# When the layer norm's tiles are normalised in a two-layer expert FFN: half 1's first norm one tile per step, half 0's second norm one step earlier

## What is computed

```python
x = x + ffn1(layernorm(x), token_ids, ctx, ctx, ctx)
x = x + ffn2(layernorm(x), Wg, W1, W2, W3)

# ffn1: 4 experts of width 256, chosen by the token's id
y = einsum('bsf,df->bsd', silu(h @ Wg[e].T) * (h @ Wu[e].T), Wd[e])   # Wg = Wu = Wd = ctx
# ffn2: 8 experts of width 176, the best 2 of 8 scores, softmax over the two
h = silu(x @ W1[e].T) * (x @ W2[e].T)
y = y + w[..., e:e + 1] * (h @ W3[e].T)
```

## Time and profile before

| | us |
|---|---|
| median of 3 runs | 166.16 |
| lowest and highest run | 165.45, 166.22 |
| span of the profiled execution | 165.1 |
| PE busy in it | 154.5 |
| DVE busy in it | 114.8 |
| POOL busy in it | 55.9 |

### The profile page before, as it was taken

One profiled execution on the slowest core, in us unless ns is written; L12 is line 12 of the kernel. 1 busy time (PEld: TensorE's weight loads), 2 busy tenths in 40 slices (PEclk: granted clock), 3 DMA queues, 4 the chain that ended last, 5 costly groups with the idle time before them and its releaser, 6 DMA issues.

```text
span 165.1 us, 2425 instructions
## 1 busy us (share of the span) xinstructions
PE 154.5 (94%) x892; PEld 131.7 (80%) x892; DVE 114.8 (70%) x225; ACT 65.1 (39%) x115; POOL 55.9 (34%) x47
## 2 busy tenths in 40 slices
PE   7599799999995999999999999999999999999991
PEld 2177689898982879888888778898888888888890
DVE  0788999955989865799999784945444744444452
ACT  3395557643742431763344432206222222222210
POOL 0599825779796330757464000000000000000000
PEclk9999999999999599999999999999999999999999
DMA  3975325232033000150000000000000300000003
GB/s 104 331 271 173 95 67 142 81 95 81 22 95 95 0 0 4 16 175 0 0 0 4 2 0 0 2 4 0 0 0 0 126 5 0 0 0 4 0 2 127
DMA packets 4332, 8.76 MB, mean 53 GB/s; under 512 B 736, under 2 KB 864, under 8 KB 4320
## 3 DMA queue, kind: packets, MB, share of 16 engines
q1 hardware_dynamic: 4176, 8.60, 16.7%
q10 hardware_dynamic: 144, 0.00, 0.0%
HBM read 7.55 MB, written 1.05 MB: 52 GB/s over the span
## 4 chain that ended last, share of the span: by engine, by line
PE 46%; DVE 17%; issue 14%; POOL 13%; ACT 4%; DMA 3%; SPq 1%; DVEq 0%; POOLq 0%; ACTq 0%
PE z L626 26%; PE y L651 18%; POOL gated L315 9%; DVE act L538 4%; DVE act_lo L503 4%; POOL w_lo L275 3%; DMA raw<-weights_dram 3%; DVE norm L436 2%; DVE x_sb L449 2%; DVE stats L421 2%; DVE gated L528 2%; ACT act_hi L352 1%; ACT w_hi L327 1%; PE y L585 1%; POOL rstd L285 1%
## 5 line engine op out<-in xcount | busy, mean ns | idle before, releaser
L626 PE MATMUL z<-hT_hi,w_hi 128*128 128x512 f32 x120 | 48.0, 400 | 0.6 <-ACT hT_hi L336 0.3
L626 PE MATMUL z<-hT_hi,w_lo 128*128 128x512 f32 x120 | 47.4, 395 | 0.0
L503 DVE TENSOR_TENSOR act_lo<-act,act_hi 128x512 fp32r<-128x512 f32 x38 | 33.4, 880 | 15.0 <-ACT act_hi L352 14.4
L651 PE MATMUL y<-w_hi,act_lo 128*128 128x256 f32 x152 | 43.5, 286 | 0.2 <-DVE act_lo L503 0.2
L651 PE MATMUL y<-w_hi,act_hi 128*128 128x256 f32 x152 | 43.5, 286 | 0.0
L651 PE MATMUL y<-w_lo,act_hi 128*128 128x256 f32 x152 | 43.4, 286 | 0.0
L380 ACT ACTIVATE silu<-z 128x512 f32<-128x512 f32 x38 | 22.7, 597 | 45.2 <-PE z L626 45.2
L626 PE MATMUL z<-hT_lo,w_hi 128*128 128x512 f32 x120 | 37.2, 391 | 0.0
L275 POOL TENSOR_TENSOR w_lo<-raw,w_hi 128x768 fp32r<-128x768 f32 (+1 forms) x15 | 27.4, 1839 | 19.3 <-ACT w_hi L327 19.3
L352 ACT CAST act_hi<-act 128x512 fp32r<-128x512 f32 x38 | 23.5, 618 | 26.0 <-DVE act L538 25.6
L651 PEld LDWEIGHTS y<-w_hi,act_lo 128*128 128x128 f32 x152 | 29.4, 193 | 2.1 <-issue 0.4
(11 more groups left out here) (48 smaller groups left out, 75.3 us busy)
## 6 DMA issues: line engine op xcount, KB each, us to landing
raw<-weights_dram SPq DMA_DIRECT2D x11, 384.0 KB, 3.2
raw<-weights_dram SPq DMA_DIRECT2D x8, 256.0 KB, 4.8
x_sb<-x_dram SPq DMA_DIRECT2D x4, 256.0 KB, 4.6
out_dram<-x_sb SPq DMA_DIRECT2D x4, 256.0 KB, 2.5
consts_sb<-consts_dram SPq DMA_DIRECT2D x1, 68.0 KB, 3.8
ids_sb<-token_ids_dram ACTq DMA_DIRECT2D x1, 4.0 KB, 4.0
router_raw<-router_dram SPq DMA_DIRECT2D x1, 8.0 KB, 2.8
```

The source lines that it names most:

```text
L503: nc.vector.tensor_tensor(act_lo[:, i, :], act[:, i, :], act_hi[:, i, :].bitcast(F32), ALU.subtract)\
L626: return nc.tensor.matmul(bank[:], w[b][:, c, cols], tokens[:, h, k, :], **flags)
L651: last = nc.tensor.matmul(o, a[:, q % BUFFERS, rows], w[b][:, c, wd], start=(first and j == 0), stop=(c == CHUNKS[b] - 1 and j == 2), skip ...
```

## The change

Four entries of the tables move, and one loop of four instructions is taken apart.

- Half 1's first norm: `normalise` no longer issues its four tiles in step 1, but one tile in each of the steps 1, 2, 3 and 4, at the place where `normalise` stood: behind that step's act and its w_lo. Its transposes move from (4, 0) to (5, 0), its `tokens_hi` from step 4 to 5, its `tokens_lo` from step 5 to 6.
- Half 0's second norm: `inverse_deviation` and `normalise` move from step 12 to step 11. Its transposes stay at step 14.
- Weight piece (1, 3) is split at step 14 and no longer at step 12: its w_hi on ACT, its w_lo on POOL.

```diff
-    "inverse_deviation": (1, 4, 5),
-    "normalise": (1, 4, 4),
-    "transpose_tokens": ((4, 0), (6, 0), (6, 1)),
-    "tokens_hi": (4, 5, 6),
-    "tokens_lo": (5, 5, 5),
+    "inverse_deviation": (1, 3, 5),
+    "normalise": (None, 3, 4),
+    "transpose_tokens": ((5, 0), (6, 0), (6, 1)),
+    "tokens_hi": (5, 5, 6),
+    "tokens_lo": (6, 5, 5),
...
-SPLIT_AT |= {6 + 2 * c: (1, c) for c in range(4)}
+SPLIT_AT |= {(6, 8, 10, 14)[c]: (1, c) for c in range(4)}
...
-                for i, t in enumerate(tiles_of(h)):
+                for i, t in [(i, h * HALF_TILES + i) for i in parts]:
...
-                    normalise(bb, hh, (x_sb, x2_sb)[bb])
+                    normalise(bb, hh, x2_sb)
+                if 1 <= q <= HALF_TILES:
+
+                    normalise(0, 1, x_sb, (q - 1,))
```

More of the change, by code:

```diff
@@ L427, in statistics, with normalise @@
                         nc.vector.tensor_scalar(var[:, cols], mv[:, cols, 1], EPS, None, ALU.add).then_inc(var_done, 1)
-            def normalise(b, h, src):
+            def normalise(b, h, src, parts=range(HALF_TILES)):
                 if ln_no(b, h):
                     dve.wait_ge(norm_T, KD * ln_no(b, h))
-                for i, t in enumerate(tiles_of(h)):
+                for i, t in [(i, h * HALF_TILES + i) for i in parts]:
                     dve.wait_ge(rstd_done, ln_part_no(ln_no(b, h), t))
```

## The result

| | before | after |
|---|---|---|
| median of 4 runs, us | 166.19 | 171.92 |
| lowest and highest run | 165.45, 166.40 | 170.73, 173.32 |
| span of the profiled execution | 165.1 | 169.9 |
| ratio, with its 95% interval | | 1.0329 (1.026 to 1.040) |

The change made the kernel 3.3% slower. I had forecast slower, 169.0 us; the time lies 2.9 us above that and 1.5 us above the range. Medians are of all runs, but a ratio, here and in the experiments, is one of mean times without the slow runs (more than 1.5% above the fastest of their kernel). Each ratio is against runs of the kernel before that were made alongside; their medians are 166.19 here, 165.94 for experiments 1 to 4, 166.25 for 5 to 8 and 166.79 for 9 to 12.

The account below looks back on a forecast made before the run. The prediction took PE, busy 154.5 of 165.1 us, as the bound. Half 1's stand +3.3, clock +1.1 and half 0's moves -1.6 put +2.8 on the median 166.16: 169.0 us, range 166.0 to 170.4.

Parts of the forecast that it names:

- The new stand of part 1: At half 1's moved transposes PE waits 4.3 us for the fourth norm tile; down(2) starts at 27.6, +3.3 us.
- the rule used for the 1.4: Old loss at half 1's transposes: 2.2 us until down(1), less 0.8 us estimated for eight transposes without a wait.
- The clock behind it: Granted clock expected to fall after half 1's long stand: +1.1 us, bounds 0 and 1.6.
- hT_lo at up(8): Half 1's later tokens_lo makes hT_lo barely due for up(8): charged nothing with the low clock, 0.3 us without.
- Part 2: Half 0's second norm at step 11, weight piece (1,3) at step 14: 3.9 us won, -1.6 us net at up(17).
- The two waits named for it: PE waits for hT_lo at the scores, 0.9 us, and for gate_rows at the gate's transposes, giving back gain.
- The anchor: Baseline of the sum: span 165.1 to 167.9 us, carried as +2.8 onto the median 166.16, giving 169.0.
- The holds: On DVE, act_lo, w_lo and norm tiles exclude POOL's gated, each for its length, four gated delaying half 1's tiles.
- The one in which the clock stays up: Rival, 22%: the clock stays full in half 1's long stand; 168.2 us (167.4 to 168.7).
- The one with fewer holds: Rival, 13%: half 1's stand costs only +1.9 with the clock up, half 0's moves bring 1.9; 166.2 us.
- the faster case: Rival, 9%: DVE's tiles slip between POOL's instructions in both places; costs 0.3, wins 3.9; 162.6 us (to 165.3).
- the worse one: Rival, 8%: a second low stretch of the clock when the scores wait, +1.6; 170.6 us.

Follow-up runs that it names:

- experiments 1 to 4: Four follow-up kernels: the change's half 1 norm alone, its other moves alone, half 0's earlier norm alone, and the changed kernel with filler matmuls; 172.48, 165.92, 166.88, 169.41 us.
- 5 to 8: Four follow-up kernels: filler in the kernel before, a two-tiles-a-step norm, a later weight piece (1,3), and filler with halved gated; 165.27, 167.33, 166.61, 168.53 us.
- 9 to 12: Four follow-up kernels: weight piece (1,3) at step 14 without and with filler, two-tiles-a-step norm with early rounding, and these combined; 164.78, 164.56, 164.47, 163.48 us.
- after_fill16: Changed kernel plus 16 throwaway matmuls in front of half 1's transposes, where PE stands anyway; 169.41 us, ratio 1.020 to the kernel before.
- part1_only: Changed kernel with half 0's second norm and weight piece (1,3) back at step 12, leaving only half 1's norm moves; 172.48 us, ratio 1.039.
- tiles22: Kernel before with half 1's norm as two tiles in steps 1 and 2, transposes and tokens moved as in the change; 167.33 us, ratio 1.002.
- part2_only: Kernel before with only half 0's second norm at step 11 and weight piece (1,3) at step 14; 165.92 us, ratio 1.001.
- the fifth experiment: The run before_warm, with its table of spans by mean granted clock; 165.27 us, ratio 0.992.
- after_fill10_halfgate: Changed kernel plus 10 filler matmuls before half 1's transposes, with gated(3) to gated(5) on half the columns; 168.53 us, ratio 1.015 to the kernel before.
- piece14_only: Kernel before with only weight piece (1,3) moved from step 12 to 14, both norms staying; 164.78 us, ratio 0.990.
- norm11_only: Kernel before with only half 0's second norm at step 11, weight piece (1,3) staying at step 12; 166.88 us, ratio 1.006.
- before_warm: Kernel before with filler matmuls in the starting warm-up and in front of half 1's first and half 0's second transposes; 165.27 us, ratio 0.992.

## Why the prediction was wrong in size and right in kind

- **The new stand of part 1** was right in its mechanism, and in its number partly by luck. Tile 4 was put at 26.97 and ended at 26.78; down(2) was put at 27.6, +3.3 us, and started at 27.81, +3.45. The 0.65 us from the last tile to down(2) was a full-clock figure and became 1.03 on the low clock. Without it, as after_fill16 shows, down(2) is 3.0 us late. (The wait, put at 4.3 us, is 4.9 - 0.8 = 4.1 by the rule used for the 1.4.)
- **The clock behind it is the term that failed**: +1.1 us with bounds of 0 and 1.6, measured +2.3 (5.16 us against 2.82), and with the 0.4 us in the stand 2.7 in all. I took the worst case from the one low stretch of before, 1.6 us, and deducted what would pass while PE stands. The low level did begin during the stand, at 26.0, but it then lasted 6.8 us and not the 3.4 of before, so 5 us of it fell on PE's work. In part1_only the same stand brought 3.4 us of it and cost 1.1. A bound from a single row was no bound.
- **hT_lo at up(8)** was charged at nothing with the low clock; down(3) to down(5) takes 0.4 us more than before, all of it in up(8), and tiles22's profile names this wait in the same place. The change moved tokens_lo behind the router's remainder, which POOL's w_lo holds.
- **Part 2** was right in the profile: forecast 3.9 won and 2.3 given back, -1.6 net; measured from down(5) to up(17) 6.20 - 4.81 = 1.4. Two misses nearly cancel in it: 3.3 won (1.8 at down(11) instead of 2.3, and 1.5 of clock, 4.43 against 2.92) and 1.9 given back. The two waits named for it are there, 0.7 and 0.6 us. But 1.6 of the 3.9 was the low clock behind the second stand, which 8 of 31 runs of before don't have anywhere. Against those, part2_only is 0.3 us slower.
- **The anchor.** The sum was made on a span of 165.1 and put on the median 166.16 as a difference. Every run has 1.8 us outside its span, so the profiled execution stood for 166.9 us, 0.7 above that median: the 11 runs with its mean clock of 0.99 in the fifth experiment's table span 164.2 to 165.0, and it is slower than each of them. The changed kernel's span and median agree (169.9 + 1.8 = 171.7, and 171.92). So +4.8 in span became +5.7 between the medians. In the span the forecast was 2.0 us too low: 1.2 by the clock, 0.4 by hT_lo, 0.2 by part 2 and 0.15 by down(2). The clock term alone would have put the time at 170.2, still inside the range; with the anchor it is outside.
- **The holds.** That DVE's w_lo waits for POOL's gated, on which the 3.3 us rest, is borne out by after_fill10_halfgate; that tiles are held by POOL's work, by piece14_only (2.02 us for four instead of 3.51). The Trainium skill ("SBUF — State Buffer", Who interferes with whom) says that a DVE instruction with two SBUF inputs contends with a GpSimd instruction that reads SBUF; the w_lo of 0.98 and 0.68 us beside the halved gated, in place of 1.18 and 1.15, agree. One reading of the prediction needs care: by the earlier trace rows the third tile starts at 18.96, before gated at 19.04, and yet it is the tile that is held, so the recorded starts don't tell which of the two got in first.
- **The rivals.** The one in which the clock stays up fell for the profiled run, and none of the four has a full clock: their spans are 168.9, 169.9, 170.3 and 171.5, at mean clocks of 0.99 to 0.967. Its 168.2 would have been too low even so, since after_fill16 has 168.8 and 168.9 at the full clock: it deducts from part 2 a clock price that such a run doesn't pay. The one with fewer holds and the faster case, both with an earlier tile 4, fell, and so did the worse one: while the scores wait the clock is full.

What is open: how much of the clock's price an execution pays in which stand, and why the same stand brought 6.8 us of low clock in one profile and 3.4 in another. I have one profile of each kernel, and the mean clock of the other runs does not say where the low stretches lie.

## What to carry to other kernels

Splitting a block of work over steps moves its last piece later. Look in the timeline when that piece will be done, and not only at its step: here the transposes moved one step (2.82 us) and the last tile 6.0 us (from 20.78 to 26.78). Two tiles a step fitted the new place; no run moved the transposes further. Taking a competitor out of the way (w_lo at step 12) gave 0.7 us at the full clock, where moving the norm itself gave nothing, since what stood behind it was pushed back. Filling TensorE's unavoidable stands with throwaway matmuls gave a ratio of 0.992 here, and ten runs that agree within 0.5 us but for one.

## What the runs showed of the hardware

- One and the same program runs from 163.2 to 168.3 us of span, mostly in groups by the mean granted clock, with 1.0, 1.3 and 2.5 us between the medians of neighbouring groups (the table of the fifth experiment). So two kernels are best compared at the same mean clock.
- The clock can also fall at the very start, in the wait for the first weights and x: in part2_only's profile it is 0.52 from 8.0 to 11.4 us, where the profile of before has 1.00 with the same instructions. The row of that stretch:

```profile
8.00:11.40 3.40, 3.40 (x14) 2.83 (x15) 3.03 (x5) 2.05 (x5) 3.04 (x2) 0.52 0.56 201
```

- rstd on POOL (128x4, a power) took 1.40 us in the changed kernel (from 52.34), where DVE's act_lo had started just ahead of it (52.17), and 1.00 before, where act_lo started just behind it (48.09 and 47.92) and itself took its usual 0.69. Part2_only, norm11_only and tiles22 have the first order and 1.39, piece14_only and before_warm the second and 1.01. So here it mattered which of the two started first.
